# Second attention layer: the mask bias moved from products on TensorE into one row of the key product

## The reference, cut to what matters

```python
q = layernorm(x) @ Wq.T                    # 16 heads of 64, from 128 channels
k, v = split(context @ Wkv.T)              # 77 keys in each batch
sim = einsum('bhid,bhjd->bhij', q, k) * SCALE
sim = where(mask[:, None, None, :], sim, -max)
attn = softmax(sim)
x = x + tanh(g) * (einsum('bhij,bhjd->bhid', attn, v) @ Wout.T + b_out)
```

## Time and profile before

| what | value |
|---|---|
| median of three runs | 1676.58 us |
| the profiled execution: its own time, its span | 1680.8 us, 1677.6 us |
| busy: TensorE, VectorE, ScalarE, GpSimd | 1537.4, 1095.2, 922.3, 625.6 us |
| mean granted TensorE clock | 0.970 |
| first attention, score products | 51.7 to 617.4 us |
| second attention, score products | 823.1 to 1506.1 us |

### The profile page before, as it was taken

One profiled execution on the slowest core, in us unless ns is written; L12 is line 12 of the kernel. 1 busy time (PEld: TensorE's weight loads), 2 busy tenths in 40 slices (PEclk: granted clock), 3 DMA queues, 4 the chain that ended last, 5 costly groups with the idle time before them and its releaser, 6 DMA issues. The chain is left out here.

```text
span 1677.6 us, 27705 instructions
## 1 busy us (share of the span) xinstructions
PE 1537.4 (92%) x9286; PEld 1212.3 (72%) x9286; DVE 1095.2 (65%) x2370; ACT 922.3 (55%) x1903; POOL 625.6 (37%) x747
## 2 busy tenths in 40 slices
PE   6999999999999974588999999999999999997996
PEld 5888888888888762287777677776777677766774
DVE  5677767777676766987645554555545554665996
ACT  3666666666666535801555555565555555545662
POOL 1233333333333336601133232323323232336995
PEclk9999999999999997989999999999999999998998
DMA  8444444444444312000533334334333333210111
GB/s 276 158 142 153 135 153 134 153 137 136 156 131 149 93 60 65 0 1 17 188 125 105 124 110 134 104 128 122 112 119 116 117 115 121 87 61 1 32 32 38
DMA packets 196284, 181.99 MB, mean 108 GB/s; under 512 B 12096, under 2 KB 193344, under 8 KB 196160
## 3 DMA queue, kind: packets, MB, share of 16 engines
q1 hardware_dynamic: 195584, 180.28, 34.1%
q10 hardware_dynamic: 576, 0.13, 0.0%
HBM read 95.43 MB, written 84.93 MB: 108 GB/s over the span
## 5 line engine op out<-in xcount | busy, mean ns | idle before, releaser
L873 POOL TENSOR_TENSOR PN<-E,RC 128x512 f32<-128x512 f32 (+1 forms) x384 | 336.2, 903 | 633.7 <-DVE RC L830 633.7
L784 DVE TENSOR_REDUCE MX<-pS 128x6 f32<-128x462 f32 (+1 forms) x384 | 223.1, 581 | 331.4 <-PE pS L553 331.2
L636 ACT ACTIVATE G<-pP 128x308 f32<-128x308 f32 x488 | 208.9, 429 | 284.0 <-PE pP L490 280.5
L588 PE MATMUL pO<-work,PT 128*128 128x128 f32 (+1 forms) x2560 | 332.6, 278 | 21.3 <-ACT PT L685 21.3
L553 PE MATMUL pS<-G,XT 128*128 128x462 f32 (+1 forms) x768 | 346.1, 534 | 0.0
L588 PEld LDWEIGHTS pO<-work,PT 128*128 128x128 f32 (+1 forms) x2560 | 310.2, 193 | 29.4 <-issue 27.6
L676 ACT ACTIVATE E<-E 128x462 f32<-128x462 f32 (+1 forms) x384 | 209.2, 545 | 151.4 <-DVE E L794 145.2
L488 PE MATMUL pP<-Chi,Ahi 128*128 128x308 f32 x496 | 240.7, 485 | 1.4 <-ACT G L636 1.2
L685 ACT ACTIVATE PT<-pT 128x512 f32<-128x512 f32 (+1 forms) x384 | 200.5, 522 | 53.4 <-PE pT L573 53.1
L794 DVE TENSOR_TENSOR E<-pS,MX 128x462 f32<-128x462 f32 (+1 forms) x384 | 223.7, 582 | 9.1 <-issue 0.2
L573 PE MATMUL pT<-ident,PN 128*128 128x128 f32 (+1 forms) x1280 | 202.4, 277 | 18.9 <-POOL PN L873 18.9
(11 more groups left out here) (197 smaller groups left out, 2042.3 us busy)
## 6 DMA issues: line engine op xcount, KB each, us to landing
values<-ST SPq DMA_DIRECT2D x256, 256.0 KB
work<-values SPq DMA_DIRECT2D x512, 128.0 KB
values<-ST SPq DMA_DIRECT2D x64, 208.0 KB
work<-values SPq DMA_DIRECT2D x128, 104.0 KB
C<-in_ctx SPq DMA_DIRECT2D x32, 154.0 KB
out<-s_O SPq DMA_DIRECT2D x16, 256.0 KB, 2.2
work<-in_L_xattn_Wq SPq DMA_DIRECT2D x2, 512.0 KB, 7.3
work<-in_L_xattn_Wkv SPq DMA_DIRECT2D x2, 512.0 KB, 7.9
```

The costliest lines, as they stand in the source:

```text
L588: last = nc.tensor.matmul(pO[:, 0:CH], PT[0:rows, c, :], V[(t - 1) % VRING][0:rows, tile, CH * hh:CH * hh + CH], start=c == 0, stop=c == C ...
L636: return nc.scalar.activation(G[:, g % 2, :, head, :], bank[:, 0:KEYCOLS].rearrange("p (b k) -> p b k", k=KEYS), ACT.Copy)
L784: nc.vector.tensor_reduce(MX[:, h0:h1], pS[u][:, 0:(h1 - h0) * KEYS].rearrange("p (h k) -> p h k", k=KEYS), X_AXIS, ALU.max).then_inc(max_ ...
L873: nc.gpsimd.tensor_tensor(out, e, scale, ALU.mult).then_inc(prob_ready, 1)
```

## The change

In the second layer the last channel of the query weights is subtracted from the other 127 in the fold (VectorE, with TensorE waiting for it by a semaphore `centred`). As the channels of a layernorm sum to zero, the first 127 channels then give the same scores without the last. The last channel of XN is set to 1.0 once, `normalise` writes only channels 0 to 126, and the copies of G write only rows 0 to 126. Row 127 of G receives the mask bias, now float32, by DMA: `place_mask(g)` issues four DMAs from SyncE for each group, each of which writes the bias of one batch 16 times (once for each head). Groups 0 and 1 are placed before the first value is sent; every later group g + 1 is placed in SyncE's iteration t = 4g + 1, after the scores of group g - 1. TensorE waits for the placing at the head of a group, and the products L552 are gone. `mask_bias` waits for the placing of two groups before in the place of the scores.

```diff
--- before.py
+++ after.py
@@ -151,6 +151,8 @@
         banks = [tmp.enter_context(nc.psum_tensor(f"fold_bank{layer}_{i}", [128, 4, 128], F32)) for i in range(4)]
         ctx_banks = [tmp.enter_context(nc.psum_tensor(f"ctx_bank{layer}_{i}", [128, 512], F32)) for i in range(2)]
         padded = tmp.enter_context(nc.semaphore(f"padded_{layer}"))
+        if layer == 1:
+            centred = tmp.enter_context(nc.semaphore("centred"))
         sem = {n: tmp.enter_context(nc.semaphore(f"{n}_{layer}")) for n in
                ("params_in", "turned", "turned_out", "folded", "hi_done",
                 "lo_done", "gate_done")}
@@ -228,6 +230,8 @@
             pe.wait_ge(sem["turned_out"], 2 * len(turn))
 
 
+            if layer == 1:
+                pe.wait_ge(centred, 1)
             for n, (left, right) in enumerate((("k", "q"), ("v", "o"))):
                 if n == 1:
                     for g in range(2):
@@ -309,6 +313,11 @@
                 for c in range(FC):
                     nc.vector.tensor_scalar(WOUT[:, c, :], WOUT[:, c, :], ROUND, inv[:, 1, c:c + 1],
                                             ALU.subtract, ALU.mult)
+            if layer == 1:
+                dve.wait_ge(loaded["q"], 16)
+                body = hd["q"][:, :, 0:CH - 1]
+                nc.vector.tensor_tensor(body, body, hd["q"][:, :, CH - 1:CH].to_broadcast([128, INNER_CHUNKS, CH - 1]),
+                                        ALU.subtract).then_inc(centred, 1)
             for n, (hi, lo, scale) in enumerate(((p["Ahi"], p["Alo"], HEAD_DIM ** -0.5), (p["Bhi"], p["Blo"], 1.0))):
                 if n == 1:
                     for g in range(2):
@@ -375,17 +384,19 @@
         RC = sb("RC", [128, 2, HEADS])
         if layer == 1:
             M8 = sb("M8", [1, 2, KEYCOLS], U8)
-            MB = sb("MB", [1, 2, KEYCOLS], BF16)
+            MB = sb("MB", [1, 2, KEYCOLS])
 
         pS = [ps(f"pS{u}", [128, 512]) for u in range(3)]
         pP = [ps(f"pP{i}", [128, 512]) for i in range(2)]
         pT = [ps(f"pT{i}", [128, 4, 128]) for i in range(2)]
         pO = ps("pO", [128, 512])
         first_banks = pP + pS[0:2]
+        live = CH if layer == 0 else CH - 1
 
         c_in, ct_turned, chi_out, clo_out, tiled = (ctx[n] for n in ("c_in", "ct_turned", "chi_out", "clo_out", "tiled"))
         if layer == 1:
             m_in, bias_ready = [sem("m_in0"), sem("m_in1")], sem("bias_ready")
+            bias_in, one_done = [sem("bias_in0"), sem("bias_in1")], sem("one_done")
         score_ready, max_done, shifted, exp_done = sem("score_ready"), sem("max_done"), sem("shifted"), sem("exp_done")
         sum_done, recip_done, prob_ready = sem("sum_done"), sem("recip_done"), sem("prob_ready")
         made, made_out, first_made = sem("made"), sem("made_out"), sem("first_made")
@@ -446,9 +457,19 @@
                     sp.dma_start(V[t % VRING][0:8 * keys, n, :], p["values"][octet % 2, n, :, b * keys:(b + 1) * keys, :]
                                  ).then_inc(v_in[t % VRING], 16)
 
+            def place_mask(g):
+
+                sp.wait_ge(bias_ready, g + 1)
+                for b in range(GROUP):
+                    sp.dma_start(G[CH - 1:CH, g % 2, b, :, :],
+                                 MB[0:1, g % 2, b * KEYS:(b + 1) * KEYS].unsqueeze(1).to_broadcast([1, HEADS, KEYS])
+                                 ).then_inc(bias_in[g % 2], 16)
+
             if layer == 1:
                 load_mask(0)
                 load_mask(1)
+                place_mask(0)
+                place_mask(1)
             for v in range(BLOCKS):
                 sp.wait_ge(first_out[v % 2], v // 2 + 1)
                 send(v)
@@ -461,6 +482,9 @@
                 if layer == 1 and t % GROUP == 0 and 1 <= group < GROUPS - 1:
                     sp.wait_ge(bias_ready, group)
                     load_mask(group + 1)
+                if layer == 1 and t % GROUP == 1 and 1 <= group < GROUPS - 1:
+                    sp.wait_ge(score_ready, group * 3 * GROUP)
+                    place_mask(group + 1)
                 if t % PAIR == 0 and t // PAIR >= 1:
                     for back in range(VRING):
                         last = t - 1 - back
@@ -478,6 +502,8 @@
         def _(pe):
             def turn_x(g):
                 pe.wait_ge(xn_done, g + 1)
+                if layer == 1:
+                    pe.wait_ge(one_done, 1)
                 for b in range(GROUP):
                     last = nc.tensor.transpose(pO[:, b * 128:b * 128 + 128], XN[:, b, :], p["ident"][:, :])
                 last.then_inc(xt_turned, 1)
@@ -544,14 +570,10 @@
                     wait(pe, shifted, (t - 1) * 3 + u + 1)
                     h0, h1 = UNITS[u]
                     out = pS[u][:, 0:(h1 - h0) * KEYS]
-                    if layer == 1:
-                        if u == 0 and b == 0:
-                            pe.wait_ge(bias_ready, group + 1)
-                        bias = MB[0:1, half, b * KEYS:(b + 1) * KEYS].unsqueeze(1).to_broadcast(
-                            [1, h1 - h0, KEYS])
-                        nc.tensor.matmul(out, p["onesb"][0:1, :], bias, start=True, stop=False)
+                    if layer == 1 and u == 0 and b == 0:
+                        pe.wait_ge(bias_in[half], 16 * GROUP * (group // 2 + 1))
                     nc.tensor.matmul(out, XT[:, half, b, :], G[:, half, b, h0:h1, :].rearrange("p h k -> p (h k)"),
-                                     start=layer == 0, stop=True).then_inc(score_ready, 1)
+                                     start=True, stop=True).then_inc(score_ready, 1)
 
                 def chunk(c):
 
@@ -633,8 +655,8 @@
                                      ACT.Copy).then_inc(xt_out, 1)
 
             def keys_out(bank, g, head):
-                return nc.scalar.activation(G[:, g % 2, :, head, :],
-                                            bank[:, 0:KEYCOLS].rearrange("p (b k) -> p b k", k=KEYS), ACT.Copy)
+                return nc.scalar.activation(G[0:live, g % 2, :, head, :],
+                                            bank[0:live, 0:KEYCOLS].rearrange("p (b k) -> p b k", k=KEYS), ACT.Copy)
 
             def values_out(bank, v):
                 rows = tile_rows(v % BLOCKS // QUARTERS)
@@ -713,7 +735,8 @@
         def _(dve):
             def mask_bias(g):
                 dve.wait_ge(m_in[g % 2], 16 * (g // 2 + 1))
-                wait(dve, score_ready, (g - 1) * 3 * GROUP)
+                if g >= 2:
+                    dve.wait_ge(bias_in[g % 2], 16 * GROUP * (g // 2))
                 nc.vector.tensor_scalar(MB[0:1, g % 2, :], M8[0:1, g % 2, :], MASKED, -MASKED,
                                         ALU.mult, ALU.add).then_inc(bias_ready, 1)
 
@@ -734,7 +757,7 @@
                 dve.wait_ge(rs_done, g + 1)
                 wait(dve, xt_turned, g)
                 for b in range(GROUP):
-                    last = nc.vector.tensor_scalar(XN[:, b, :], p["X"][:, g * GROUP + b, :], MV[:, b, 0:1],
+                    last = nc.vector.tensor_scalar(XN[:, b, 0:live], p["X"][:, g * GROUP + b, 0:live], MV[:, b, 0:1],
                                                    RS[:, b:b + 1], ALU.subtract, ALU.mult)
                 last.then_inc(xn_done, 1)
 
@@ -755,6 +778,8 @@
 
             if layer == 0:
                 dve.wait_ge(p["x_in"][0], 16)
+            else:
+                nc.vector.memset(XN[:, :, live:CH], 1.0).then_inc(one_done, 1)
             statistics(0)
             normalise(0)
             if layer == 1:
@@ -768,8 +793,8 @@
                     wait(dve, sent[n % RING], 16 * (n // RING))
                     nc.vector.tensor_copy(ST[0:rows, n % RING, :], bank[0:rows, :]).then_inc(first_out[1], 1)
                 else:
-                    nc.vector.tensor_copy(G[:, 0, :, n - BLOCKS, :],
-                                          bank[:, 0:KEYCOLS].rearrange("p (b k) -> p b k", k=KEYS)
+                    nc.vector.tensor_copy(G[0:live, 0, :, n - BLOCKS, :],
+                                          bank[0:live, 0:KEYCOLS].rearrange("p (b k) -> p b k", k=KEYS)
                                           ).then_inc(first_out[1], 1)
 
             def slot(t):
```

## The result

The changed kernel takes 1613.81 us (median of four runs, 1611.9 to 1617.94) against 1677.38 us of the kernel before in the same comparison: a ratio of 0.9619, interval 0.9596 to 0.9643, 63.6 us less. A second comparison gave 1613.51 against 1678.68 us, 0.961 (0.9595 to 0.9625). The forecast was 1609, with a range of 1598 to 1632.

A forecast was written before the change was run, and what follows sets the result against it. TensorE was taken as the busiest engine in both attentions. Products -73.5, clock +4, start +1.5, fold +0.3 and small edits +0.1 sum to -67.6 us: a median of 1609.0, range 1600 to 1618, 8-in-10 range 1598 to 1632.

The forecast's parts named there:

- The products, -73.5 us: Second layer's score stretch: 117.3 us over the first layer's, less 43.8 for seven stalls, leaves 73.5 us gained.
- The other way, 57 slots of 1.44 us: Second layer's slots that aren't stalled: 1.44 us gained in each of 57, 82 us in all, kept for the bound.
- The stalled slots give nothing: Seven slots waiting for late mask bytes: removed products only lengthen TensorE's wait, from 2.24 to about 3.7 us.
- The clock, +4 us: Behind the seven stalls: longer waits may prolong TensorE's low clock, 0.6 us each, +4 us; bounds 0 to 10.5.
- The start, +1.5 us: Second attention's start: first send 4.1 to 5.4 us later behind the placings, mostly covered; +1.5 us, bounds 0 and 5.4.
- The fold's +0.3: In the fold: VectorE's subtraction takes 1.2 us, partly covered by TensorE's context wait; +0.3 us, bounds 0 and 1.2.
- The placings in the slots, nothing: SyncE in 14 groups: four more issues, 1.2 to 2.5 us each time, covered by its waits for ScalarE; cost nothing.
- Half credit: Rival, second layer's slots: removed products return only their own step, 48 us, giving 1635; chance 0.12 together with the isolated-spacing estimate.
- The recorded estimate by the isolated spacing: Removed products priced at 195 ns for 462 columns: some 29 us over 57 slots, giving 1653; chance 0.12 with half credit.
- The colder TensorE: Rival, seven stalls: a second low-clock stretch, 1.5 us each, giving 1615, or 1620 with others elsewhere; chance 0.12.
- A move of the bound to VectorE's chain: Rival, no effect: VectorE's chain bounds once the products go, slots stay at 10.6 us, some 1677; chance 0.02.
- The slower case: Rival: SyncE's placings delay sends and fetches, TensorE waits for values in 14 groups, loss over 5 us; chance 0.03.

The follow-up runs named there:

- experiment 1: The kernel before with the mask products alone left out, so the mask isn't applied: 1609.19 us, ratio 0.9574.
- Experiment 2: The changed kernel with the placings of groups 0 and 1 moved behind the 20 first sends: 1609.83 us, ratio 0.9584.
- 10: The changed kernel run once more, unaltered, beside the others on one chip: 1613.51 us.
- Experiments 3 and 4: All mask bytes loaded by one transfer: 3 in the changed kernel, 1568.09 us; 4 in the kernel before, 1646.66 us.

## Why the prediction was right, point by point

**Direction, size and mechanism: right.** 1609.0 was said, 1613.8 measured; the gain was 63.6 us where 67.6 was forecast. That the sum came this close is partly luck: the term of the clock was too large, that of the start too small, and the two errors have opposite signs.

**The products, -73.5 us: right.** The stretch fell by 74.3 us in the profiled pair; experiments 1, 2 and 10 give 71.2, 71.2 and 72.9. The value came from taking the first layer as the model of what is left. The other way, 57 slots of 1.44 us, was kept as a bound and is too high, for the reason given there. Experiments 3 and 4 show it without stalls as well: 64 slots of 1.44 would be 92 us, and it is 83.4, because the slots with few pieces (t % 8 = 7, and the last nine) gain only 0.5 to 1.2 us.

**The stalled slots give nothing: right.** Seven stalls remained (12.95 to 16.69 us where about 15 to 16 was said), TensorE's wait grew by 1.4 us in each on average, and experiments 3 and 4 isolate their loss at 9.1 us.

**The clock, +4 us: the row was read rightly and the term was too large.** The low clock follows six of the seven stalls of the profiled changed kernel, and its total didn't grow clearly: the seven stalls cost 42.2, 43.6, 45.3 and 45.3 us over the 566.5, where I had 43.8 + 4. The longer wait doesn't always bring the low clock. Slot 52 of the changed kernel has it nowhere:

```profile
1342.70:1355.60 12.90, 9.75 (x58) 7.80 (x57) 8.25 (x21) 5.83 (x14) 4.84 (x6) 1.00 0.32 107
```

It takes 12.95 us with a wait of 2.6 us for GpSimd; slot 12 takes 3.5 us more with a wait 1.3 us longer. The low clock is then worth some 2.2 us in slot 12, an estimate from these numbers. What decides whether it falls in a given slot, no run tells.

**The start, +1.5 us: too small, 3.5 measured.** The step that failed is the sentence that ST's six buffers let TensorE run ahead of the sends, and with it a cost that the term doesn't have: the low clock behind TensorE's own wait. The issue price was at the upper bound I gave (0.63 us against 0.62), but all eight issues stood in one row behind the first bias, where I had counted the last four behind the second: counted from the first mask bias the first send goes out 6.7 us later (1.2 us ahead of it before, 5.4 behind it after), not 4.1 to 5.4. The ring was full by then, a wait of 4.54 us on VectorE and ScalarE, and TensorE, ahead by less than that, stood still for 2.33 us. The nine products behind it follow each other after 0.43 us in place of 0.23, some 1.6 us more (an estimate from the rows' starts). Together that is a little more than the 3.5 us that reached the first score. Experiment 2 removes all of it. The fold's +0.3 measured 0.4; VectorE's subtraction was priced from the row sum by columns, 1.2 against 1.15 us.

**The placings in the slots, nothing: right.** Each takes SyncE 0.59 us in the median and lands 2.4 us later; the slots of the changed kernel that don't stall equal the first layer's to 0.04 us in their medians, for each t % 8.

**The rivals.** Half credit is refuted by experiment 1: the neighbours' part belongs to the products. The recorded estimate by the isolated spacing that the Trainium skill gives ("TensorE: Matmul & The Clock Gate", "Back-to-back issue gap") comes to an estimate of 0.52 us for the three products of a slot. The trace agrees roughly for a product over all rows (0.58) but not for one row (1.44). The colder TensorE stayed under 2 us over the 43.8. A move of the bound to VectorE's chain is ruled out by slots of 9.19 us. The slower case never had a place: no wait of TensorE for a placing or for late values appears.

In the profiled pair the terms nearly add up. The stretch was 4.8 us better than -73.5 + 4, the start 2.0 worse, the fold 0.1 and the end 0.7 worse; with the 2.7 us ahead of the first layer's first score that isn't the change's, the span fell by 67.1 us against the 67.6 forecast. The medians are 63.6 and 65.2 us apart in the two comparisons. The profiled run of the kernel before, 1680.8 us, was 2 to 4 us above its medians, that of the changed kernel, 1612.9, about 1 below. The remaining difference is the spread of single runs, and no run tells where in the program it lies.

## What to carry to other kernels

A small product next to large ones is not priced by its busy time: compare start to start with a stretch that lacks it. If it contracts over 64 rows or fewer, take it out, or pad it with zeros to 128 (a product of zeros over 128 rows stands for this here; a padded product that does the mask's work was not run). And where a chain hangs on a tiny transfer queued behind large ones, load it early and once: here 308 bytes a group cost 42 us, over half of what the whole change gained. New transfers belong behind the ones that a ring of buffers waits for.

## What the runs showed of the hardware that was not expected

A bf16 product over 1, 32 or 64 rows between float32 products over 128 rows cost the slot the same, 1.41 to 1.43 us for three of them; over 128 rows it cost 0.58. Products over 78 and 104 rows show no such loss. The loss lies on both sides of the small product, about 0.1 us before and 0.1 us behind each, besides a longer step to the score (0.30 us against 0.21). In float32 over one row the three cost 3.2 us. An issue from SyncE of a transfer whose source is one row read 16 times took 0.59 us, about as long as a fetch of 128 KB (0.57) and twice the 0.31 us of the 308-byte load.
